# Two layers of routed experts on one core: first-layer low weights on GpSimd, a router chain in three parts, wider router products, and other waits in the last sums

## The reference

```python
# layer 0
w_bot = einsum('bg,got->bot', y, weight * mask)
h = einsum('bnt,bot->bno', x, w_bot) + bias
probs = softmax(h @ router_w.T)
topk_vals, topk_idx = top_k(probs, 2)
topk_w = topk_vals / (topk_vals.sum(-1) + 1e-06)
x = x + sum_k (h @ expert_weights[topk_idx_k] + probs[topk_idx_k]) * topk_w_k
# layer 1
h = x @ W_base.T + b_base + 2 * sum_e w[b, e] * (x @ As[e].T) @ Bs[e].T
w, sel = top_k(softmax(h @ gate_w), 2); w = w / w.sum(-1)
x = x + sum over 2 shared experts of swiglu(h) + sum over the chosen of w * swiglu(h)
```

## Time and profile before

| | |
|---|---|
| median of 3 runs | 363.57 us (362.91 to 364.14) |
| the profiled execution | 362.66 us |
| its span | 360.9 us |
| TensorE (PE) busy | 350.2 us, 97% |
| VectorE (DVE) busy | 236.0 us, 65% |
| ScalarE (ACT) busy | 165.8 us, 46% |
| GpSimd (POOL) busy | 135.9 us, 38% |
| granted TensorE clock | 1.00 |
| chain that ended last | PE 77%, DVE 10%, DMA 4%, ACT 3% |

### The profile page before, as it was taken

The page is one execution under the profiler, slowest core; times in us unless marked ns, Lnnn a source line. Parts: engine busy times, 40 slices in busy tenths (PEclk is TensorE's granted clock), DMA queues, the critical chain, the costliest instruction groups (busy, mean ns, idle before and its releaser), DMA issues.

```text
span 360.9 us, 8032 instructions
## 1 busy us (share of the span) xinstructions
PE 350.2 (97%) x2788; PEld 218.8 (61%) x2789; DVE 236.0 (65%) x595; ACT 165.8 (46%) x285; POOL 135.9 (38%) x220
## 2 busy tenths in 40 slices
PE   7998999999999999989999999999999999999996
PEld 2553544455455455547447777777777777766655
DVE  1357999967666762779987555565555555665596
ACT  1036384677577457544342233333433333324393
POOL 4000534863773674000002365555555555432000
PEclk9999999999999999999999999999999999999999
DMA  7994125244434521010002345345345443211963
GB/s 208 380 373 160 61 76 155 83 152 136 120 113 137 154 77 60 0 61 2 0 0 98 101 163 190 118 161 203 116 153 195 132 154 116 73 45 42 329 241 118
DMA packets 21962, 47.43 MB, mean 131 GB/s; under 512 B 3120, under 2 KB 12080, under 8 KB 21808
## 3 DMA queue, kind: packets, MB, share of 16 engines
q1 hardware_dynamic: 17760, 37.63, 30.5%
q0 software_dynamic: 3456, 9.44, 8.3%
q10 hardware_dynamic: 720, 0.02, 0.1%
HBM read 29.25 MB, written 8.91 MB: 106 GB/s over the span
## 4 chain that ended last, share of the span: by engine, by line
PE 77%; DVE 10%; DMA 4%; ACT 3%; issue 2%; SPq 1%; POOL 0%; DVEq 0%; POOLq 0%; ACTq 0%
PE bank L1115 55%; PE bank L1126 7%; PE bank L1283 4%; PE bank L1385 3%; PE bank L1139 3%; PE bank L1360 2%; DMA w1s<-results 2%; DVE x L833 2%; ACT w1s L615 2%; SPq L438 1%; DMA x<-wc 1%; ACT sil L626 1%; PE bank L1199 1%; DVE prod L1008 1%; DVE hs L691 1%
## 5 line engine op out<-in xcount | busy, mean ns | idle before, releaser
L492 POOL TENSOR_TENSOR w1s<-piece,w1s 128x170 f16<-128x170 f32 x128 | 61.6, 518 | 78.3 <-ACT piece L577 78.3
L1115 PE MATMUL bank<-w0s,hs 128*128 128x512 f16 x384 | 86.2, 380 | 1.2 <-DVE x L833 1.2
L833 DVE SCALAR_TENSOR_TENSOR x<-bank,coef,x 128x256 f32<-128x256 f32 x128 | 54.8, 477 | 19.4 <-PE bank L1115 19.1
L501 POOL DMA_INDIRECT rows<-token_store,row_in x36 | 35.0, 971 | 79.3 <-DVE row_in L953 47.0
L1115 PEld LDWEIGHTS bank<-w0s,hs 128*128 128x128 f16 x384 | 36.9, 98 | 43.9 <-DVE x L833 1.8
L1115 PE MATMUL bank<-hs,w1s 128*128 128x512 f16 x264 | 59.3, 380 | 0.9 <-DVE prod L1008 0.8
L1115 PE MATMUL bank<-w1s,rT 128*128 x336 | 54.5, 313 | 0.0
L507 POOL DMA_INDIRECT results<-yb,row_out x36 | 35.7, 991 | 35.9 <-ACT yb L664 35.9
L1115 PEld LDWEIGHTS bank<-hs,w1s 128*128 128x128 f16 x264 | 25.2, 98 | 30.2 <-DVE prod L1008 2.2
L658 ACT ACTIVATE ract<-prod 128x352 f16<-128x352 f32 x36 | 17.9, 496 | 53.9 <-DVE prod L1086 45.6
L1115 PEld LDWEIGHTS bank<-w1s,rT 128*128 128x128 f16 x336 | 31.7, 98 | 14.6
(11 more groups left out here) (175 smaller groups left out, 475.5 us busy)
## 6 DMA issues: line engine op xcount, KB each, us to landing
piece<-w SPq DMA_DIRECT2D x16, 680.0 KB, 3.9
xrow<-w1s SPq DMA_DIRECT2D x8, 704.0 KB
xrow<-w1s SPq DMA_DIRECT2D x8, 384.0 KB
w1s<-results SPq DMA_DIRECT2D x6, 512.0 KB, 7.5
x<-wc SPq DMA_DIRECT2D x4, 512.0 KB, 6.9
w1s<-xT SPq DMA_DIRECT2D x4, 512.0 KB, 11.0
w1s<-w SPq DMA_DIRECT2D x4, 512.0 KB, 9.4
token_store<-xrow SPq DMA_DIRECT2D x4, 512.0 KB, 3.1
```

What stands on the lines that cost most here:

```text
L492: ins = nc.gpsimd.tensor_tensor(w1s[:, LO, at], piece[:, i % 2, part], w1s[:, HI, at], ALU.subtract)
L501: pool.indirect_dma_start(rows[:, i % 2], None, token_store, bass.IndirectOffsetOnAxis(row_in[:, slot_tile(i):slot_tile(i) + 1], 0)).then_ ...
L833: nc.vector.scalar_tensor_tensor(x1[:, t], bank[(n + a) % 4][:, h * D:(h + 1) * D], coef[:, t, e:e + 1], x1[:, t], ALU.mult, ALU.add).then ...
L1115: mm = nc.tensor.matmul(out_ap, l, r, start=(i == 0), stop=(i == len(terms) - 1))
```

## The change

The low weights of layer 0 move from VectorE to GpSimd, with a scaled f32 copy on ScalarE. The router chain of layer 0 runs in three parts (tiles 0 to 3, 4 to 7, 8 to 15). The router weights lie with HI and LO side by side, so that one matmul of 16 columns replaces two of 8 (four instead of six for a tile, the LO*LO product now in it), and VectorE's copy becomes a sum of the two halves. Router products and LoRA steps move in their queues. Each transfer of the end has a semaphore of its own, and the first final sum stands between accumulations.

```diff
-        rs = sb("rs", [P, 2, 2, KT, E], F16)
+        rs = sb("rs", [P, 2, KT, 2, E], F16)
-        s_yg = [sem(f"s_yg{c}") for c in range(B)]
+        s_yg = [[sem(f"s_yg{c}{k}") for k in range(K_TOP)] for c in range(B)]
-        PARTS = [slice(0, TPB), slice(TPB, NT)]
+        PARTS = [slice(0, TPB), slice(TPB, 2 * TPB), slice(2 * TPB, NT)]
+        LORA = {1: 0, 2: 1, 4: 2, 6: 3}
+        def lora_bank(b):
+            return bank[7 if b < 2 else 4]
...
         @block.gpsimd
+            for j in range(PAIRS):
+                pool.wait_ge(sm["s_w0sc"], j + 1)
+                for k in range(KT):
+                    for n in range(PW // P):
+                        at = slice(j * PW + n * P, j * PW + (n + 1) * P)
+                        ins = nc.gpsimd.tensor_tensor(w0s[:, LO, k, at], w0_in[j][:, k, n * P:(n + 1) * P],
+                                                      w0s[:, HI, k, at], ALU.subtract)
+                ins.then_inc(sm["s_w0lo"], 1)
...
         @block.scalar
+            def w0_scaled(j):
+                act.wait_ge(sm["s_w0hi"], j + 1)
+                nc.scalar.activation(w0_in[j], w0_in[j], ACT.Copy, scale=SW).then_inc(sm["s_w0sc"], 1)
             h_hi(0, 0)
             w0_hi(0)
             h_hi(0, 1)
+            w0_scaled(0)
+            w0_hi(1)
             exps(0, PARTS[0], 1.0 / (SH0 * SW))
+            w0_scaled(1)
             h_hi(0, 2)
-            w0_hi(1)
+            w0_hi(2)
+            w0_scaled(2)
             h_hi(0, 3)
-            w0_hi(2)
             w0_hi(3)
+            w0_scaled(3)
...
             for m in range(TWO):
-                if m == 1:
-                    exps(1, PARTS[1], 1.0 / (SH0 * SW))
+                if m in (1, 3):
+                    exps((m + 1) // 2, PARTS[(m + 1) // 2], 1.0 / (SH0 * SW))
...
-                if m < B:
-                    wl_hi(m)
+                if m in LORA:
+                    wl_hi(LORA[m])
...
+                if m == 3:
+                    act.wait_ge(sm["s_r0"], 3)
                 if m + 1 < TWO:
                     add_bias(2 * m + 2)
                     add_bias(2 * m + 3)
...
             def scaled(o, part):
-                act.wait_ge(s_yg[c], 16 * K_TOP)
+                act.wait_ge(s_yg[c][k], 16)
...
         @block.vector
-            def w0_lo(j):
-                dve.wait_ge(sm["s_w0hi"], j + 1)
-                cols = slice(j * PW, (j + 1) * PW)
-                nc.vector.scalar_tensor_tensor(w0s[:, LO, :, cols], w0_in[j], SW, w0s[:, HI, :, cols],
-                                               ALU.mult, ALU.subtract).then_inc(sm["s_w0lo"], 1)
...
             def take_logits(layer, part, tiles):
-                dve.wait_ge(sm["s_log"], 5 if layer else 2 * part + 1)
-                at = bank[6 + layer][:, tiles.start * E:tiles.stop * E].rearrange("p (t e) -> p t e", e=E)
-                ins = nc.vector.tensor_copy(lg[:, tiles], at)
-                ins.then_inc(sm["s_lg"], 1)
-                dve.wait_ge(sm["s_lg"], 2 * layer + part + 1)
+                dve.wait_ge(sm["s_log"], 5 if layer else part + 1)
+                at = bank[6 + layer][:, 2 * tiles.start * E:2 * tiles.stop * E].rearrange("p (t a e) -> p t e a", a=2, e=E)
+                nc.vector.tensor_reduce(lg[:, tiles], at, AX.X, ALU.add).then_inc(sm["s_lg"], 1)
+                dve.wait_ge(sm["s_lg"], 3 * layer + part + 1)
...
             h_lo(0, 1)
-            w0_lo(0)
             largest(PARTS[0])
             second(PARTS[0])
             shares0(0, PARTS[0])
             h_lo(0, 2)
-            w0_lo(1)
...
                     if m == 0 and j == 0:
                         h_lo(0, 3)
-                        w0_lo(2)
-                    if m == 0 and j == 1:
-                        w0_lo(3)
-                    if m == 1 and j == 2:
-                        shares0(1, PARTS[1])
+                    if m == 0 and j == 2:
+                        dve.wait_ge(sm["s_lw"], 48)
+                        lora_scaled(0)
+                        lora_scaled(1)
+                    if m == 1 and j == 0:
+                        take_logits(0, 2, PARTS[2])
+                    if m in (1, 3) and j == 2 - m // 2:
+                        shares0((m + 1) // 2, PARTS[(m + 1) // 2])
...
                 if m == 0:
                     take_logits(0, 1, PARTS[1])
-                    largest(PARTS[1])
-                    second(PARTS[1])
+                if m in (0, 2):
+                    largest(PARTS[m // 2 + 1])
+                    second(PARTS[m // 2 + 1])
...
             def accumulate(c):
+                    if c == 2 and q == 1:
+                        combine(0, range(TPB // 2))
+                    if c == 2 and q == 2:
+                        combine(0, range(TPB // 2, TPB))
...
                 if i == 3 * ST:
-                    for n in range(FIRST_SUM):
-                        combine(n)
+                    combine(1)
...
         @block.tensor
             def logits(layer, c):
-                    mm = group(bank[6 + layer][:, t * E:(t + 1) * E],
-                               [(hs[:, a, k, t * P:(t + 1) * P], rs[:, layer, b, k, :])
-                                for k in range(KT) for a, b in PASSES])
+                    mm = group(bank[6 + layer][:, 2 * t * E:2 * (t + 1) * E],
+                               [(hs[:, a, k, t * P:(t + 1) * P], rs[:, layer, k].rearrange("p a e -> p (a e)"))
+                                for k in range(KT) for a in (HI, LO)])
...
-                if c >= 1:
+                if c in (1, 2):
                     logits(0, c - 1)
...
             def lora(b):
+                if b >= 2:
+                    pe.wait_ge(sm["s_rows"], (b - 1) * TPB)
...
             def transposes(m):
                 if m == 0:
                     pe.wait_ge(sm["s_bias"], 2)
-                    pe.wait_ge(sm["s_lg"], 2)
+                    pe.wait_ge(sm["s_lg"], 3)
...
             def layer1_input(c):
+                pe.wait_ge(sm["s_wlf"], min(c + 2, B))
...
-                    if m < B and j == (m == 0):
-                        lora(m)
-                    if m == 0 and j == 1:
-                        logits(0, B - 1)
+                    if m in LORA and j == 0:
+                        lora(LORA[m])
+                    if m == 0 and j < 2:
+                        logits(0, 2 + j)
```

More of the change, by code:

```diff
@@ L229, in build_program @@
             "s_w0hi",
+            "s_w0sc",
             "s_w0lo",
@@ L438, in _ @@
                     sp.dma_start(yg[c][:, k], results[at:at + S, :].rearrange("(t p) d -> p t d", p=P)
-                                 ).then_inc(s_yg[c], 16)
+                                 ).then_inc(s_yg[c][k], 16)
             for c in range(B - 1):
@@ L644, in _ @@
                 if i == ST + 1:
-                    exps(2, ALL, 1.0 / (SH1 * SW))
+                    exps(3, ALL, 1.0 / (SH1 * SW))
             def step(s, par):
@@ L720, in _ @@
             dve.wait_ge(sm["s_rsp"], 1)
-            nc.vector.scalar_tensor_tensor(rs[:, :, LO].rearrange("p a k e -> p a (k e)"),
-                                           rin[:].rearrange("p a k e -> p a (k e)"), SW,
-                                           rs[:, :, HI].rearrange("p a k e -> p a (k e)"),
-                                           ALU.mult, ALU.subtract).then_inc(sm["s_rsp"], 1)
+            parts = rs[:].rearrange("p l k a e -> p (l k) a e")
+            nc.vector.scalar_tensor_tensor(parts[:, :, LO], rin[:].rearrange("p l k e -> p (l k) e"), SW,
+                                           parts[:, :, HI], ALU.mult, ALU.subtract).then_inc(sm["s_rsp"], 1)
             masked(2)
@@ L804, in wl_sum @@
                 dve.wait_ge(sm["s_lora"], b + 1)
-                nc.vector.scalar_tensor_tensor(wl[:, b % 2], wb_in[:], SWC, bank[7][:], ALU.mult,
+                nc.vector.scalar_tensor_tensor(wl[:, b % 2], wb_in[:], SWC, lora_bank(b)[:], ALU.mult,
                                                ALU.add).then_inc(sm["s_wlf"], 1)
-                if b + 1 < B:
-                    lora_scaled(b + 1)
             def wl_lo(b):
@@ L837, in _ @@
                         h_lo(0, 3)
-                        w0_lo(2)
-                    if m == 0 and j == 1:
-                        w0_lo(3)
-                    if m == 1 and j == 2:
-                        shares0(1, PARTS[1])
+                    if m == 0 and j == 2:
[6 more added lines that the diff above has]
+                        shares0((m + 1) // 2, PARTS[(m + 1) // 2])
                     if j == 0 and m >= 3 and m % 2 == 1:
                         h_lo(1, (m - 3) // 2)
-                    if j == 1 and m < B:
-                        wl_sum(m)
+                    if j == 1 and m in LORA:
+                        wl_sum(LORA[m])
                     if j == 2 and m >= 1:
                         tr_lo(m - 1)
-                if m < B:
-                    wl_lo(m)
+                if m in LORA:
+                    wl_lo(LORA[m])
+                if m in (3, 5):
```

(14 more changed lines are left out.)

6 lines of the change are left out of this document (1 added, 5 removed).

## The result

| | before | after |
|---|---|---|
| median | 363.24 us (362.51 to 364.14) | 359.07 us (357.66 to 359.82) |
| the profiled execution | 362.66 us, span 360.9 | 359.82 us, span 358.0 |
| TensorE busy | 350.2 us | 348.6 us |
| VectorE, ScalarE, GpSimd busy | 236.0, 165.8, 135.9 us | 238.5, 170.1, 147.5 us |

The account below looks back on a forecast made before the run. TensorE was taken as the bound. Ended waits 3.5 and router products 1.4, less new waits 1.85, then -0.13 and +0.23, make 3.2 us: 362.66 becomes 359.5, the median 360.4, range 358.4 to 363.5.

Parts of the forecast that it names:

- What bounds the kernel: TensorE waits little, so ending its waits or giving it less work wins; its early idle stretches together cost 3.5 us.
- The first gap: TensorE's idle 1.81 us between layer 0's projections and the next product goes; new idle of 0.45 us replaces it.
- T: In layer 0, h_lo behind VectorE's chain for tiles 0 to 3 was forecast to end at 31.0+14c=33.1.
- c: Mean wait of a two-SBUF-input VectorE chain operation beside GpSimd: 0.15 us; the gain is 7.4-28c.
- The port rival: GpSimd and VectorE block each other's SBUF port longer: 364.6 us at c=0.3, the gain turning at c=0.26; chance 0.09.
- The three parts: Splitting layer 0's router chain adds TensorE waits: 0.35 for the logits' bank, 0.1 for m=2's bank, 0.95 for token rows.
- Router products: Sixteen 16-column products take 0.41 us a group for 0.61: 0.2 for each of seven groups before 147.9, 1.4 us.
- layer 1's sum: VectorE's copy of 128 logits becomes a sum over 256 PSUM columns: 0.42 or 0.28 for 0.28, counted as -0.13 us.
- the eighth group: The router group whose shortening gains nothing, since from 150.56 VectorE's chain for layer 1 sets the pace.
- The tail: At the end, a semaphore a transfer removes ScalarE's 0.23 wait at 344.61: 0.23 us gained, bounded by 0.4.
- The rival that said so: The new end does nothing, another transfer being late instead: 0.23 less, inside the forecast's own range, chance 0.50.
- The step that failed: Converting to the median: the profiled 362.66 lies 0.9 under the median 363.57, so 359.5 becomes 360.4.

Follow-up runs that it names:

- its two nearest versions: The changed kernel with twelve warm-up products instead of eight (358.30 us, 0.9856), and the changed kernel with the end of before (0.9862).

## Why the prediction was right in its walk and short in its size

- **What bounds the kernel** held: TensorE is still busy 97% of its span, and the lead at layer 1's first products (3.0 us with the start taken off) is 2.9 at the first routed product and 2.9 at the last down product.
- **The first gap**: 1.81 gone, 0.19 in its place where 0.45 was written. T, the end of h_lo, was 32.66 for 33.1, since the chain started at 24.32 for 24.5 and lasted 7.0 for 7.2.
- **c** was written as 0.15; the chain's 1.9 us over 14 operations make 0.14. The port rival (its chance 0.09), which needed 0.26, was refuted at 128 columns. At 512 its mechanism is there: the chain takes 8.3 us, and TensorE waits 1.33 for h_lo.
- **The three parts**: waits of 0.43, 0.39 and 0.61 for 0.35, 0.1 and 0.95. Together with the first 1.62 for 1.85: the places right, the sizes within 0.35.
- **Router products**: 0.40 a group for 0.41, 1.4 in seven groups; **layer 1's sum** 0.41 for 0.42 against 0.28. Ahead of layer 1's ranks TensorE now waits 1.01, where 0.7 stood: the eighth group was covered, as said.
- **The tail**: 0.23 forecast, nothing measured. The failed step took that wait of ScalarE for one whose end shortens the run; it went, and a wait of 0.35 for another transfer came. The rival that said so held.
- **The sum against the traced execution**: 3.2 forecast, 2.84 measured, or 2.9 from first projection to first routed product, where the tail has no part. Its one surplus term is the tail.
- **The step that failed** is the last of the sum: the profiled run "lies 0.9 under the median 363.57, which becomes 360.4". That took what the profile lacked for an offset which both kernels share. It isn't shared. The kernel before loses 1.7 us in 73 executions of 104 to a fall of TensorE's clock behind its first idle stretch, and the profile read was of one without it, but with the late start of 1.5 us, which made it look near the median. The change takes the idle stretch away, so the price of that gap was 1.81 in the profile and 3.5 where the clock falls. In none of 21 executions of the changed kernel and its two nearest versions does it fall. With the trace's 2.9 it makes 4.6.

That the fall exists, that it goes when the idle stretch is filled, which gains 1.8 (0.9 to 2.8), and comes back with the stretch, at a cost of 4.0, is shown. That it makes up the difference between traced and timed gain is shown with twelve warm-up products, where only three executions have the fall. With eight it is an estimate: 1.7 us in seven executions of ten is 1.2 of the 2 us. The rest is within the interval of the ratio, and the start and the 0.6 us behind the first routed product may hold a part of it. Why the clock falls in one execution and not in the next is open.

## What to carry over

An idle stretch of TensorE early in a kernel can cost its own length and, in some executions, a stretch at the lower clock behind it; look at the clock in several profiles, and at the mean clock of every timed execution, before the price of a gap is taken from one. Where the work can't be moved into such a gap, useless products in it may pay. When GpSimd works beside a chain of VectorE operations with two SBUF inputs, cut GpSimd's instructions short, and move the operations that nobody waits for, and the waits ahead of them, behind the ones somebody does.

## What the runs showed of the hardware

- TensorE's idle stretch of 1.6 us and more was followed by a granted clock of 0.50 to 0.61 for 3 us in four profiles of nine, and by none in the others; the idle 1.33 us with GpSimd's 512 columns by none in five executions. Idle stretches of 0.7 to 1.0 us later in the run were followed by one in no profile.
- In the first 5 us, and with a late start up to 9 or 10, the view gives the granted clock as 1.00, though the eight warm-up products take 3.60 us, 0.43 apart, the spacing of the 1.2 GHz level, and the mixing products' records last as long as theirs (631 ns). A clock of 1.00 there is no proof of the upper level; the spacing of equal products, or the mean of one, is the better row.
- GpSimd's subtraction takes 0.40 us for 128 columns and 1.13 for 512: by these two 0.16 of it is fixed (an estimate), so short instructions cost GpSimd 0.5 us in 512 columns, and still the kernel is faster with them.
- Sixteen-column products come 25 ns apart, the same as eight-column ones: between these two widths a product's columns cost nothing here.
